# A fused recurrence, attention and expert block on one core: a decay recurrence with one difference for its exponents, keys' halves stacked by transfers, and normalisations on ScalarE

## The reference

```python
# layer 1: time mixing. w = -exp(time_decay), u = time_first, v = r
k = einsum('btc,hc->bth', x, Wk); r = einsum('btc,hc->bth', x, Wr); v = r
# per channel, over the time steps:
q = max(pp, u + kt); e1 = exp(pp - q); e2 = exp(u + kt - q)
y = (e1 * a + e2 * vt) / (e1 * b + e2)
q2 = max(pp + w, kt); e1b = exp(pp + w - q2); e2b = exp(kt - q2)
a, b, pp = e1b * a + e2b * vt, e1b * b + e2b, q2
x = x + einsum('bth,ch->btc', sigmoid(r) * y, Wo)
# layer 2: attention over the 16 heads of one token (not over time), then 8 experts
h = rmsnorm(layernorm(x)); q = h @ Wq + bq; kv = ((h @ Wdown + bdown) @ Wup + bup)
att = softmax(q k^T / sqrt(32)) over the heads; x2 = layernorm(x) + att v @ Wo + bo
h2 = rmsnorm(x2); gate = softmax(h2 @ Wg + bg)
out = x + x2 + sum_e gate_e * (h2 @ We_e)
```

## Time and profile before

| what | value |
|---|---|
| median of 3 runs | 3334.51 us (3332.51 to 3334.67) |
| profiled execution: its time | 3332.17 us |
| profiled execution: its span | 3330.3 us |
| TensorE busy | 2887.2 us (87%) |
| VectorE busy | 2476.6 us (74%) |
| ScalarE busy | 956.6 us (29%) |
| GpSimd busy | 686.1 us (21%) |
| granted clock of TensorE, mean | 0.941 of full speed |

### The profile page before, as it was taken

One profiled execution on the slowest core, in us unless ns is written; L12 is line 12 of the kernel. 1 busy time (PEld: TensorE's weight loads), 2 busy tenths in 40 slices (PEclk: granted clock), 3 DMA queues, 4 the chain that ended last, 5 costly groups with the idle time before them and its releaser, 6 DMA issues.

```text
span 3330.3 us, 53600 instructions
## 1 busy us (share of the span) xinstructions
PE 2887.2 (87%) x18864; PEld 1791.2 (54%) x18864; DVE 2476.6 (74%) x4548; ACT 956.6 (29%) x1823; POOL 686.1 (21%) x745
## 2 busy tenths in 40 slices
PE   2359999998888989989998898999889998999889
PEld 2235555554555655555564555555555555555544
DVE  5797777778777768777777777768777777877753
ACT  2243232322332322322331332232233232232320
POOL 0111222212122212222221222221222221212210
PEclk9669999999999999999999999999999999999999
DMA  6011111101111101111111111111111110111110
GB/s 192 15 24 20 33 33 26 30 24 33 20 33 27 33 20 33 20 33 26 33 27 26 20 33 30 29 26 27 27 26 33 27 33 20 32 21 33 26 20 13
DMA packets 588333, 102.96 MB, mean 31 GB/s; under 512 B 556562, under 2 KB 556690, under 8 KB 588050
## 3 DMA queue, kind: packets, MB, share of 16 engines
q1 hardware_dynamic: 588068, 99.40, 16.4%
HBM read 48.49 MB, written 16.78 MB: 20 GB/s over the span
## 4 chain that ended last, share of the span: by engine, by line
PE 62%; DVE 23%; issue 7%; SPq 5%; DMA 2%; ACT 0%; POOL 0%; DVEq 0%; ACTq 0%; POOLq 0%
PE bank L1049 49%; PE bank L1201 6%; DVE mcol L954 4%; SPq L424 4%; DVE zz L865 3%; PE bank L1079 3%; DVE ks L943 3%; DVE wkv L839 2%; PE bank L1191 2%; DMA qs<-m 2%; DVE acc L1028 1%; DVE wkv L827 1%; PE bank L1165 1%; DVE ht L935 1%; DVE zz L832 1%
## 5 line engine op out<-in xcount | busy, mean ns | idle before, releaser
L1049 PE MATMUL bank<-w_e,h2t 128*128 128x512 f16 x6144 | 1479.4, 398 | 19.1 <-DVE acc L1028 19.1
L1049 PEld LDWEIGHTS bank<-w_e,h2t 128*128 128x128 f16 x6144 | 617.9, 103 | 757.5 <-issue 123.1
L1028 DVE SCALAR_TENSOR_TENSOR acc<-bank,gates,acc 128x512 f32<-128x512 f32 x512 | 373.6, 737 | 164.7 <-PE bank L1049 163.6
L1201 PEld LDWEIGHTS bank<-vp,pr 128*128 128x128 f32 x2048 | 263.9, 197 | 24.0 <-DVE hrow L970 3.9
L1201 PE MATMUL bank<-vp,pr 128*128 128x33 f32 x2048 | 259.7, 275 | 3.8 <-ACT pr L608 2.7
L608 ACT ACTIVATE pr<-bank,col 128x512 f32<-128x512 f32 x256 | 171.9, 685 | 316.1 <-PE bank L1191 315.7
L865 DVE RECIPROCAL zz<-zz 128x256 f32<-128x256 f32 x128 | 219.1, 1733 | 46.8 <-POOL zz L462 46.8
L1049 PE MATMUL bank<-w_o,xo 128*128 128x512 f16 x768 | 174.3, 384 | 58.8 <-DVE xo L799 58.8
L455 POOL TENSOR_TENSOR e<-wkv 128x512 f32<-128x512 f32 x64 | 72.1, 1127 | 645.6 <-DVE wkv L827 645.6
L1191 PE MATMUL bank<-qs,ks 106*128 106x128 f16 x1024 | 104.5, 236 | 113.9 <-DMA qs<-m 113.9
L1182 PE MATMUL bank<-ks,qs 104*128 104x128 f16 x1024 | 90.8, 231 | 125.7 <-DMA ks<-k 65.7
(11 more groups left out here) (177 smaller groups left out, 3918.1 us busy)
## 6 DMA issues: line engine op xcount, KB each, us to landing
qs<-qo SPq DMA_DIRECT2D x384, 64.0 KB, 3.0
xk<-in_attn_x SPq DMA_DIRECT2D x32, 512.0 KB, 3.9
x<-in_attn_x SPq DMA_DIRECT2D x32, 512.0 KB, 3.6
result<-acc SPq DMA_DIRECT2D x32, 512.0 KB, 2.8
ks<-k SPq DMA_DIRECT2D x128, 64.0 KB, 3.0
w_e<-in_ffn_We SPq DMA_DIRECT2D x7, 1024.0 KB, 13.8
qs<-m SPq DMA_DIRECT2D x256, 2.0 KB, 1.7
qs<-in_attn_Wk SPq DMA_DIRECT2D x1, 1024.0 KB, 5.5
```

What stands on the lines that cost most here:

```text
L1028: V.scalar_tensor_tensor(out=acc[:, s, :], in0=moe_bank[u % 2][:, :], scalar=gates[:, s, e:e + 1], in1=acc[:, s, :], op0=ALU.mult, op1=ALU ...
L1049: ins = nc.tensor.matmul(dst, left(a), right(b), start=(n == 0), stop=(n == last))
L1201: ins = nc.tensor.matmul(att_bank[ATT_BANK["PV", k]][:, n * (HD + 1):(n + 1) * (HD + 1)], pr[:, k % 2, n * P:(n + 1) * P], vp[:, 4 * k + n ...
```

## The change

All of it at once: (1) In the recurrence, one difference d = k - pp (the maximum before the step) on VectorE feeds everything: both decays are exp(-relu(d + e)) and exp(-relu(-d - e)) with e = exp(time_decay), so four Relu and two Exp on ScalarE per half, and the bonus exponent is min(d + u, 64). GpSimd's two differences go. (2) y is a quotient of sums, (a + z v) / (b + z): two products with v on VectorE (`mix_value`), the numerator's sum on GpSimd. (3) The high half of k is stacked by 8 transfers on SyncE's queue, between q's low half and k's low half, in place of `att_stack`. (4) The attention values (4 per tile) and the four normalisations (8 instructions per tile) go to ScalarE as scale and bias; VectorE makes the biases (-mean x rstd). (5) `ORDER` moves `att_rest`, `mix_rec`, `mix_scan` 1 and `mix_num` 1, and adds `mix_value`.

```diff
-ZMAX = 87.0
+ZMAX = 64.0
...
 ORDER = [
-    ("moe", 1), ("att_turn", 0), ("att_rest", 0), ("mix_k", 0), ("att_latent", 0), ("att_q", 0),
-    ("att_up", 0), ("mix_v", 0), ("mix_decay", 0), ("att_stack", 0), ("moe", 2), ("mix_exp", 0),
-    ("mix_sum", 0), ("att_vt", 0), ("moe", 3), ("mix_rec", 0), ("mix_rec", 1), ("mix_scan", 0), ("moe", 4),
+    ("moe", 1), ("att_turn", 0), ("mix_k", 0), ("att_latent", 0), ("att_q", 0),
+    ("att_up", 0), ("mix_v", 0), ("mix_decay", 0), ("moe", 2), ("mix_exp", 0),
+    ("mix_sum", 0), ("mix_value", 0), ("att_vt", 0), ("att_rest", 0), ("moe", 3), ("mix_scan", 0), ("moe", 4), ("mix_rec", 0), ("mix_rec", 1),
...
-    ("mix_sum", 1), ("mix_rec", 2), ("pre_load", 0), ("att_scores", 3), ("moe", 9), ("att_probs", 2),
-    ("att_scores", 4), ("att_probs", 3), ("att_scores", 5), ("moe", 10), ("att_probs", 4), ("mix_rec", 3),
-    ("att_scores", 6), ("mix_scan", 1), ("att_probs", 5), ("att_scores", 7), ("moe", 11), ("att_probs", 6),
-    ("att_probs", 7), ("att_back", 0), ("moe", 12), ("moe", 13), ("mix_num", 1), ("mix_gate", 1),
+    ("mix_sum", 1), ("mix_value", 1), ("pre_load", 0), ("att_scores", 3), ("moe", 9), ("att_probs", 2),
+    ("att_scores", 4), ("att_probs", 3), ("att_scores", 5), ("moe", 10), ("mix_scan", 1), ("att_probs", 4), ("mix_rec", 2),
+    ("att_scores", 6), ("mix_num", 1), ("mix_rec", 3), ("att_probs", 5), ("att_scores", 7), ("moe", 11), ("att_probs", 6),
+    ("att_probs", 7), ("att_back", 0), ("moe", 12), ("moe", 13), ("mix_gate", 1),
...
@@ SyncE, att_up @@
-                for src, dst, name, first in ((qo16, qs, "q", (0, 1)), (k16, ks, "k", ())):
-                    rest = 2 if first else 1
+                for src, dst, name, first in ((qo16, qs, "q", (0, 1)), (k16, ks, "k", (0, 2))):
+                    rest = 3 - sum(first)
...
@@ GpSimd, mix_decay @@
-            def mix_decay(t, h):
-                nc.gpsimd.tensor_tensor(e1[:, :, :], wkv[:, 0, :, 0:T], wkv[:, 0, :, 1:T + 1], ALU.subtract).then_inc(mix_pool.sem, 1)
-                nc.gpsimd.tensor_tensor(e2[:, :, :], k32[:, HF * h:HF * h + HF, :], wkv[:, 0, :, 1:T + 1], ALU.subtract)\
...
@@ GpSimd, mix_num @@
+            def mix_num(t, h):
+                pool.wait_ge(*mix_dve.done(t, f"a_{h}"))
+                nc.gpsimd.tensor_tensor(ev[:, :, :], wkv[:, 1, :, 0:T], ev[:, :, :], ALU.add).then_inc(mix_pool.sem, 1)
...
@@ ScalarE, mix_exp @@
-                act.wait_ge(*mix_dve.done(t, f"zc_{h}"))
+                act.wait_ge(*mix_dve.done(t, f"dd_{h}"))
+                for c in range(HF):
+                    nc.scalar.activation(e1[:, c, :], e2[:, c, :], ACT.Relu, bias=ecol[:, HF * h + c:HF * h + c + 1]).then_inc(mix_act.sem, 1)
+                act.wait_ge(*mix_dve.done(t, f"z_{h}"))
+                act.wait_ge(*mix_act.done(t, f"ra_{h}"))
+                for c in range(HF):
+                    nc.scalar.activation(e2[:, c, :], e2[:, c, :], ACT.Relu, bias=wcol[:, HF * h + c:HF * h + c + 1], scale=-1.0)\
+                        .then_inc(mix_act.sem, 1)
+                nc.scalar.activation(e1[:, :, :], e1[:, :, :], ACT.Exp, scale=-1.0).then_inc(mix_act.sem, 1)
+                act.wait_ge(*mix_act.done(t, f"rb_{h}"))
+                nc.scalar.activation(e2[:, :, :], e2[:, :, :], ACT.Exp, scale=-1.0).then_inc(mix_act.sem, 1)
                 nc.scalar.activation(zz[:, :, :], zz[:, :, :], ACT.Exp).then_inc(mix_act.sem, 1)
...
@@ ScalarE, att_norm @@
+            def att_norm(t, _):
+                act.wait_ge(*att_dve.done(t, "shift"))
+                for s in range(SUB):
+                    nc.scalar.activation(h_rows[:, s, :], x1[t.par][:, s, :], ACT.Identity, bias=nb2[:, 1, s:s + 1], scale=rs2[:, 1, s:s + 1])\
+                        .then_inc(att_act.sem, 1)
...
@@ ScalarE, att_up @@
+                for b in range(CB):
+                    act.wait_ge(*att_pe.done(t, f"V{b // 2}"))
+                    nc.scalar.activation(va32[:, :, b, :], att_bank[ATT_BANK["V", b // 2]][:, (b % 2) * T:(b % 2) * T + T]
+                                         .rearrange("p (g j) -> p g j", g=G), ACT.Identity, bias=bvcol[:, b:b + 1], scale=colof["vv"])\
...
@@ VectorE, mix_value @@
+            def mix_value(t, h):
+                V.tensor_tensor(ev[:, :, :], zz[:, :, :], vh, ALU.mult).then_inc(mix_dve.sem, 1)
+                V.tensor_tensor(e2[:, :, :], e2[:, :, :], vh, ALU.mult).then_inc(mix_dve.sem, 1)
...
@@ VectorE, att_norm @@
+                for n in range(2):
+                    V.scalar_tensor_tensor(out=nb2[:, n, :], in0=mv2[:, :, 0], scalar=-1.0, in1=rs2[:, n, :], op0=ALU.mult, op1=ALU.mult)\
...
@@ VectorE, att_stack @@
-            def att_stack(t, _):
-                for f in range(4):
-                    for n in (0, 2):
-                        V.tensor_copy(ks[n * HD:(n + 1) * HD, :, f, :],
-                                      grouped(k16, 0)[f * HD:(f + 1) * HD].rearrange("p g b j -> p g (b j)")).then_inc(att_dve.sem, 1)
```

More of the change, by code:

```diff
@@ L394, in pre_load @@
                 if t.back(1):
[L395 to L396 removed]
+                    sp.wait_ge(*mix_dve.done(t.back(1), "dd_1"))
                 sp.dma_start(xk_rows, rows(x, t)).then_inc(x_in.sem, 16)
@@ L529, in _, with pre_norm @@
                 split_block(n)
+            def pre_norm(t, _):
+                act.wait_ge(*pre_dve.done(t, "shift"))
+                for s in range(SUB):
+                    nc.scalar.activation(xk_rows[:, s, :], xk_rows[:, s, :], ACT.Identity, bias=nb1[:, s:s + 1], scale=rs1[:, s:s + 1])\
+                        .then_inc(pre_act.sem, 1)
             def mix_turn(t, _):
@@ L621, in att_square, with att_norm2 @@
                                          accum_out=msq[:, s:s + 1]).then_inc(att_act.sem, 1)
+            def att_norm2(t, _):
+                act.wait_ge(*att_pool.done(t, "rms"))
+                for s in range(SUB):
+                    nc.scalar.activation(h_rows[:, s, :], x2[:, s, :], ACT.Copy, scale=rs3[:, s:s + 1]).then_inc(att_act.sem, 1)
             def att_turn2(t, _):
@@ L635, in moe_gate @@
                 nc.scalar.activation(gl[:, :, :], gl[:, :, :], ACT.Exp).then_inc(gate_act.sem, 1)
-            pipeline(act, {"mix_turn": mix_turn, "mix_k": mix_k, "mix_v": mix_v, "mix_exp": mix_exp,
+            pipeline(act, {"pre_norm": pre_norm, "att_norm": att_norm, "att_rest": att_rest, "att_norm2": att_norm2, "mix_turn": mix_turn, "mix_k": mix_k, "mix_v": mix_v, "mix_exp": mix_exp,
                            "mix_num": mix_num, "mix_split": mix_split, "att_turn": att_turn,
@@ L811, in pre_norm @@
                 dve.wait_ge(*pre_pool.done(t, "rstd"))
-                for s in range(SUB):
-                    V.tensor_scalar(xk_rows[:, s, :], xk_rows[:, s, :], mv1[:, s, 0:1], rs1[:, s:s + 1],
-                                    ALU.subtract, ALU.mult).then_inc(pre_dve.sem, 1)
+                V.scalar_tensor_tensor(out=nb1[:, :], in0=mv1[:, :, 0], scalar=-1.0, in1=rs1[:, :], op0=ALU.mult, op1=ALU.mult)\
+                    .then_inc(pre_dve.sem, 1)
             def mix_turn(t, _):
@@ L986, in att_project @@
                                            in1=x2[:, s, :], op0=ALU.mult, op1=ALU.add).then_inc(att_dve.sem, 1)
-            def att_norm2(t, _):
-                dve.wait_ge(*att_pool.done(t, "rms"))
-                for s in range(SUB):
-                    V.tensor_scalar(h_rows[:, s, :], x2[:, s, :], rs3[:, s:s + 1], None, ALU.mult).then_inc(att_dve.sem, 1)
             def att_turn2(t, _):
@@ L1175, in att_max @@
                     pe.wait_ge(*stack_in.done(t, "qk"))
-                    pe.wait_ge(*att_dve.done(t, "stack"))
                     if not t.back(1):
```

136 lines of the change are left out of this document (57 added, 79 removed).

## The result

The changed kernel takes **3539.43 us** (median of 4 runs, 3538.4 to 3543.99) beside 3333.51 us for the kernel before on the same chip (median of 4, 3330.87 to 3334.67): a ratio of 1.062, 95% interval 1.060 to 1.064. The forecast was 3513 us with a range of 3400 to 3595.

The account below looks back on a forecast made before the run. TensorE bounds the kernel, a pass hanging on L (stacked keys landed) and S (maxima landed). A to E sum to +6.0 us a pass, +186 over 31 passes, less 6 for G: 3513 us, range 3400 to 3595.

Parts of the forecast that it names:

- A: L, the instant the stacked keys have landed: eight added transfers on SyncE's queue make it later, +6.1 us a pass.
- B: From L to S, when the maxima have landed: VectorE, relieved of copies, values and normalisations, is ready, -1.2 us a pass.
- C: `att_norm`: two small VectorE instructions, then two of 631 ns on ScalarE, end later, +0.5 us a pass.
- D: Behind S: the wait for S grows to about 4 us and `moe` 8 runs slower, +0.3 us a pass.
- E: Second half, between the sums of `moe` 10 and 11: reordered scans and reciprocals on VectorE, +0.3 us a pass.
- G: The fill, before the first projection: the shorter recurrence saves 6 us once.
- The upper bound's second stall: On SyncE's queue: a second stall of 1.66 us like that of L417's four transfers, putting L at +7.3 us.
- F: `pre_norm`, `att_norm2`, `att_rest`, values and GpSimd: hidden by slack or the longer wait for L, counted at nothing.
- the first: At L: the added transfers are cheap and VectorE's relief shows, faster at 3276 us; chance 0.06.
- the second: On SyncE's queue: L417's four slow transfers were the copies' doing, clock stays up, 3376 us; chance 0.12.
- The third: ScalarE's `mix_exp` 1 comes late behind added Relu and Exp, TensorE waits 2 us more, 3575 us; chance 0.10.
- The fourth: Over a pass: A comes within 0.3 us of what B to E give back, time within 0.2%; chance 0.02.

Follow-up runs that it names:

- kernel 9: The change, with each of the eight added transfers carrying 32 KB in place of 64 KB from the second pass on: 3503.02 us, ratio 1.051.
- kernel 10: The change, with the 64 KB of each of the eight added transfers as one long piece for each partition: 3494.25 us, ratio 1.049.
- kernel 4: The change, with the eight transfers of k's high half issued from ScalarE's queue in place of SyncE's: 3693.98 us, ratio 1.108.
- kernel 1: The change, with k's high half copied by VectorE as before, leaving 16 transfers: 3379.66 us, ratio 1.014.
- kernel 6: kernel 1, with the attention values scaled on VectorE again as before: 3347.18 us, ratio 1.005.
- kernel 5: kernel 1, with the first half's two reciprocals moved behind the maxima in VectorE's order: 3303.15 us, ratio 0.991.

## Why the prediction was right

The direction, the place and the main term were right, the forecast 26 us low. By its steps, in us a pass, measured as means over the passes of the table of stretches:

| step | predicted | measured | by |
| --- | --- | --- | --- |
| A, transfers: L | +6.1 (3.9 to 7.3) | +6.55 | `mix_k` to L 36.32, was 29.77 |
| B, VectorE relieved: S - L | -1.2 (-2.8 to -0.4) | -1.27 | L to S 15.28, was 16.55 |
| C, `att_norm` on ScalarE | +0.5 (0 to 1.0) | +0.3 | 0.60 in every second pass |
| D, clock behind S | +0.3 (0 to 1.2) | +0.7 | S to `mix_turn` 45.52, was 44.81; 0.55 of it `moe` 8 |
| E, `ORDER`, second half | +0.3 (0 to 1) | 0 | no such wait among TensorE's |
| clock behind `mix_turn` | not in the sum | +0.4 | 8.89 us in the other passes, was 8.14 |
| sum | 6.0 | 6.7 | 105.82, was 99.11 |

The time is 206 us longer, 6.6 for each of 31 passes. G, the fill, is small: before the first projection TensorE now waits 54.32 us, 3.8 less, and goes on 2.3 us earlier (126.29 against 128.59), not 6. That the sum came within 0.7 us is in part luck: A, D and the clock behind `mix_turn` together were 1.2 us too low or left out, and C and E 0.5 too high.

**A, nearly right: +6.1, measured +6.55.** It took the eight at the mean of the last tile, 0.76 each. They take 5.96 us in the pass shown, 0.74 each, but the four behind them take 3.40 in place of 2.75. TensorE starts 2.5 us after the end of the last issue, 2.67 before. The upper bound's second stall came in part. The reason given for 0.76, that eight times 64 KB at 87 GB/s leave the engines little room, held only in half: by kernels 9 and 10 the issuing, 0.63 us each, is the greater part, 5.0 of the 6.5 us. The number was near because both ceilings are.

**B, right in the number.** It holds two parts that go against each other: VectorE is ready, and TensorE is slower behind L. Rows by stretch, first of the kernel before from S on, then of the change from L on and from S on (entries as in kernel 4):

```profile
1577.38:1582.30 4.92, 4.92 (x23) 2.65 (x23) 4.13 (x6) 1.97 (x4) 2.27 (x2) 0.65 0.02 3
```

```profile
1760.29:1766.00 5.71, 5.71 (x35) 3.50 (x36) 2.64 (x5) 0.00 (x0) 0.00 (x0) 0.66 0.00 1
...
1775.73:1781.60 5.87, 5.87 (x23) 2.83 (x23) 0.48 (x2) 4.52 (x9) 0.00 (x0) 0.53 0.31 92
```

Behind L the clock is 0.66 after 9.3 us of idling, and `moe` 5 takes 3.84 us, where it took 2.75.

**D, mis-sized: +0.3, measured +0.7.** That a longer wait for S would go with a lower clock was right: in the mean the wait grew from 3.20 to 3.85 us and `moe` 8 from 4.42 to 4.97. In the passes shown the granted clock behind S was 0.65 before and is 0.53 now, so most of `moe` 8 runs at 1.2 of the two levels of 1.2 and 2.4 GHz. But the step read a price off two rows, 4.04 us after a wait of 2.79 and 5.27 after 3.94, and took a quarter of their difference. Two other passes of the kernel before show that the length of the wait doesn't give the price:

```profile
1676.95 1.03 PE L1191 MATMUL bank<-qs,ks 106*128 106x128 f16 x8 [4.22 <-DMA qs<-m]
1677.77 3.75 PE L1049 MATMUL bank<-w_e,h2t 128*128 128x512 f16 x12
...
1772.73 1.03 PE L1191 MATMUL bank<-qs,ks 106*128 106x128 f16 x8 [4.26 <-DMA qs<-m]
1773.56 5.33 PE L1049 MATMUL bank<-w_e,h2t 128*128 128x512 f16 x12
```

The same wait, and `moe` 8 takes 3.75 us in one and 5.33 in the other.

**Left out: the clock behind `mix_turn`.** In every second pass TensorE waits 3 to 4 us ahead of the transposes of x, before and now. What follows got slower. First before, then in the change, where the last line is the pass after:

```profile
1623.68 1.09 PE L1079 MATMUL bank<-ident,xk 128*128 128x128 f32 x8 [3.38 <-issue]
1624.60 5.34 PE L1049 MATMUL bank<-w_e,h2t 128*128 128x512 f16 x24
```

```profile
1713.89 1.96 PE L1077 MATMUL bank<-ident,xk 128*128 128x128 f32 x8 [3.22 <-issue]
1715.65 7.39 PE L1047 MATMUL bank<-w_e,h2t 128*128 128x512 f16 x24
...
1826.24 1.09 PE L1077 MATMUL bank<-ident,hrow 128*128 128x128 f32 x8 [0.44 <-ACT hrow L582]
```

From these transposes to those of h it took 6.1 to 9.0 us before and takes 8.7 to 9.1 now. The prediction had no term for it, and what moved the clock there is not shown.

**C, nearly right.** The pair on ScalarE is dearer than the 631 ns that I took (805 ns each, with a bias and a scale for every partition), but only one pass of every two has a wait for it, 0.44 us, and the transposes of h come 0.60 us later in it (the last line above).

**F, right for the change, and by its cover only.** Values and the normalisations other than `att_norm` show no wait of TensorE's as long as the keys come 6.5 us late. The step named that cover for the wait on the maxima. Kernels 1 and 6 show the price without it: 0.6 us a pass between L and S for the values (1.05 in the whole time). The reciprocals ahead of the maxima, which stood there before too, cost 2.5 once the keys are early (kernel 5). VectorE's load fell by 13.8 us a pass, where the prediction said some 16.

Of the rivals, the first (cheap transfers) and the second (the slow four are the copies' doing) are out: the four of L417 take 4.64 us with no copy beside them. The third (ScalarE late in the second half) did not happen: the waits above hold none for ScalarE's second exponentials. The fourth (it cancels) is out with A at 6.55 against 1.27 given back.

My own expectation for kernel 1 was wrong in a way that is worth more than the forecast. I took the change without transfers to give 68 us back, since VectorE loses 428 us of work. But between Q and the maxima, where the pass hangs on it, the change puts relus and values ahead of ScalarE's exponentials, the adds of `att_rest` on GpSimd beside a pair of scans, and leaves two pairs of scans and two reciprocals ahead of the maxima, where they were. And it adds 0.7 us a pass between `mix_turn` and `mix_k`, which I had not looked at.
